# Copying the last depthwise unit of a chunk in two halves, and letting the first scores wait for the first half alone

## The chip, the cores and the metric

The kernel runs on one core of one Trainium2 chip. The metric is device time in microseconds (us) of that core; lower is better. All arithmetic is float32. Five queues of instructions run side by side and meet at semaphores: PE (TensorE, matmuls; PEld in the views is its weight load), ACT (ScalarE), DVE (VectorE), POOL (GpSimd, which only clears one small tile here) and SP (SyncE, which issues the transfers). Each executes its own instructions in the order written.

## The reference, cut to what matters

The input is x of (4, 64, 128, 128). It is group-normalised (32 groups of 2 channels), goes through a windowed channel attention, and is added back:

```python
x + attention(_gn(x))
qkv = einsum('bchw,oc->bohw', x, w_qkv) + b_qkv           # 64 -> 192 channels
qkv = depthwise_3x3(qkv, w_dw) + b_dw                     # padded by 1
# windows of 8x8 pixels, 4 heads of 16 channels, pixels flattened to 64
attn = softmax(einsum('nhcx,nhdx->nhcd', q, k) * temperature)
out  = einsum('nhcd,nhdx->nhcx', attn, v)
gate = gelu(einsum('nhcx,yx->nhcy', v, w_mlp) + b_mlp)
out  = einsum('bchw,oc->bohw', unwindow(out * gate), w_proj) + b_proj
```

## The kernel before, in words

Two images at a time fill the 128 partitions, so there are two pairs of images, each cut into 8 bands of 16 rows: 16 chunks. A chunk has 16 columns of windows, and one window column stands for 4 "patches" of the tile `qkv` (2 rows of windows by 2 images), 64 patches in all. A chunk is worked off in four steps of 4 window columns (16 patches) each; the step has number i, the chunk is i // 4, and a = i % 4 is the place in the chunk. There are 64 steps.

The work on a chunk has two layers, and the kernel does both at once.

**The lower layer makes q, k and v of the next chunk.** It is cut into 22 units. Sixteen `mix` units (8 in step a=0, 8 in step a=1; `mix_channels`, matmuls of L672) multiply the normalised patches by the 64 to 192 channel weights. Six `dw` units (three in step a=2, three in step a=3; `depthwise`, matmuls of L707) apply the 3x3 filter as a 64-column matmul per channel, 32 matmuls to a unit. A unit writes one of two PSUM buffers of two banks each (`work`; units take them in turn), raises `full` of the buffer, is copied to SBUF, and the copy raises `free`. The copies are `evacuate_mix` (to `z`) and `evacuate_dw` (to `qkv`), on ACT except for one unit per chunk. Units 0 and 1 of `dw` hold v, 2 and 3 hold q, 4 and 5 hold k: unit 5 brings 16 of the channels of k for all 64 patches, and is the last of the chunk. It is in the second buffer, which the unit after the next one, mix 1 of the following chunk, takes again.

**The upper layer is the attention of the current chunk**, one step at a time: `score` (L744, 64x64 products of q and k), on DVE the mask, the maximum and its subtraction (L511, L516, L518), on ACT the exponential (`exponent`, L341), on DVE sum, reciprocal, product and transpose (L532 to L543); `turn_v` (L777, a transpose of v) with its copy on ACT (`v_up`, L347); `gates` (L765) for two steps at a time with `gate_up` on DVE (L525) and `gelu` on ACT (L351); `apply_probs` (L793), `mix` on DVE (L503), `project` (L804) and `residual` (L552).

The order of each engine is written out by hand. At a chunk's start PE does this: `depthwise` of units 4 and 5 of the coming chunk, `apply_probs` of the last step, `qkv_of` (two waits: units 4 and 5 are copied), `score` of step a=0, mix 0 and mix 1, `project` of the step before, `turn_v`, mix 2 to mix 5, `gates`, `apply_probs`, mix 6 and 7. In the very first step, mix 0, mix 1 and the gates stand between `qkv_of` and `score`.

ACT does in step a=3: the exponential, the copy of unit 3, `v_up`, the table of Gelu, the Gelu of one step, the copy of unit 4, the Gelu of a second step, the copy of unit 5, and the table of the exponential (`exp_table`, L356: the load and a one-element activation). Then in step a=0: the copies of mix 0 and mix 1, the exponential, `v_up`, and the copies of mix 2 to 5. A Gelu and an exponential need different tables, so each change costs an ACT_TABLE_LOAD.

For the first chunk (n = 0) units 0, 2 and 4 are copied by ACT and 1, 3 and 5 by DVE (L417 is its copy helper, L326 that of ACT). The semaphores that the change touches are `free[1]`, raised by the copy of unit 5, and a new one.

Of the kernel before, what the change touches and what calls it, by code (L numbers as in the profile page):

```python
# [26 lines left out]
NW = 4 * COLS  # L27
BATCH = 4
BATCHES = COLS // BATCH
# [12 lines left out]
SPLIT = 16  # L42
# [44 lines left out]
def gates_in(i):  # L87

    return (i + 2, i + 3) if i % 2 == 0 and i + 2 < STEPS else ()


def gelus_in(i):

    a = i % BATCHES
    return (0, 1) if i == 0 else (i, i + 1) if a == 2 else gates_in(i - 1) if a == 3 else ()
# [7 lines left out]
def build(nc, x, taps, hot, edges, weights, out):  # L103
    with ExitStack() as ctx:
        def sb(name, shape, dt=F32):
            return ctx.enter_context(nc.sbuf_tensor(name, shape, dt))
# [4 lines left out]
        def sem(name):  # L111
            return ctx.enter_context(nc.semaphore(name))

        z = sb("z", [P, QKV, NW])
        dw = sb("dw", [P, QKV, HW])
        qkv = sb("qkv", [P, 2, 3, NW, HALF])
# [19 lines left out]
        at = [sum(sizes[:n]) for n in range(len(sizes) + 1)]  # L136
# [11 lines left out]
        work = [unit_ps[:, 0:2], unit_ps[:, 2:4]]  # L148
# [19 lines left out]
        free = [sem("free0"), sem("free1")]  # L168
# [9 lines left out]
        deviated = sem("deviated")  # L178
        seen_done = sem("seen_done")
        patches_ready = sem("patches_ready")  # L180
        gate_done = sem("gate_done")
        scores_done = sem("scores_done")
        v_t_done = sem("v_t_done")
# [21 lines left out]
        def wait_full(engine, unit):  # L205
            engine.wait_ge(full[number[unit] % 2], number[unit] // 2 + 1)

        def wait_free(engine, unit):
            engine.wait_ge(free[number[unit] % 2], number[unit] // 2 + 1)

        def buffer(unit):
            return number[unit] % 2
# [5 lines left out]
        def evacuate_first(engine, copy, g):  # L218

            engine.wait_ge(first_full[g % 4], g // 4 + 1)  # L220
            copy(z[0:NPATCH, :, 4 * g:4 * g + 4].rearrange("p c (b t) -> p c b t", t=2),
                 quarter[g % 4][0:NPATCH, :, 0:2 * QKV].rearrange("p t (b c) -> p c b t", b=2)
                 ).then_inc(first_free[g % 4], 1)

        def evacuate_mix(engine, copy, n, g):

            unit = ("mix", n, g)
            wait_full(engine, unit)
            copy(z[0:NPATCH, :, 4 * g:4 * g + 4].rearrange("p c (b t) -> p c b t", t=2),
                 work[buffer(unit)][0:NPATCH, :, 0:2 * QKV].rearrange("p t (b c) -> p c b t", b=2)  # L230
                 ).then_inc(free[buffer(unit)], 1)

        def evacuate_dw(engine, copy, n, v):

            unit = ("dw", n, v)
            if n > 1:
                engine.wait_ge(v_t_done, (n - 1) * BATCHES)
            wait_full(engine, unit)
            kind, at = kind_of(v)
            copy(qkv[:, n % 2, kind, :, at:at + SPLIT],  # L240
                 work[buffer(unit)][:].rearrange("p a (c w) -> p w (a c)", w=NW)
                 ).then_inc(free[buffer(unit)], 1)

        def kind_of(v):
            return (2, 0, 1)[v // (HALF // SPLIT)], v % (HALF // SPLIT) * SPLIT
# [73 lines left out]
        @block.scalar  # L319
        def _(act):  # L320
            act.dma_start(tap_w[:], taps).then_inc(taps_in, 16)
            act.dma_start(hot_b, hot).then_inc(hot_in, 16)
            act.dma_start(consts[:], weights).then_inc(consts_in, 16)

            def copy(to, of):
                return nc.scalar.activation(to, of, ACT.Copy)  # L326

            def evacuate_build(m):

                act.wait_ge(built, m + 1)  # L330
                px = PX * TILES
                copy(dw[0:K, :, m * px:(m + 1) * px].rearrange("p c (r x) -> p c r x", x=PX),
                     banks[m % 2][0:K, :, 0:PX * QKV].rearrange("p r (x c) -> p c r x", x=PX)).then_inc(dw_ready, 1)

            def deviation(pair):
                wait_free(act, ("var", pair))
                nc.scalar.activation(small[:, 3:4], small[:, 2:3], ACT.Sqrt).then_inc(deviated, 1)

            def exponent(i):
                act.wait_ge(shifted, i + 1)  # L340
                nc.scalar.activation(scores[:], scores[:], ACT.Exp).then_inc(exp_ready, 1)  # L341

            def v_up(i):
                act.wait_ge(v_t_done, i + 1)
                if i:
                    act.wait_ge(mix_done, i)
                nc.scalar.activation(v_t[:], turn_ps, ACT.Copy).then_inc(v_t_ready, 1)  # L347

            def gelu(j):
                act.wait_ge(gate_biased, j + 1)  # L350
                nc.scalar.activation(gate[:, j % GATES], gate[:, j % GATES], ACT.Gelu).then_inc(gate_ready, 1)  # L351

            def exp_table(k):
                if k:
                    act.wait_ge(table_loaded, k)
                nc.scalar.activation(small[:, 7:8], zeros[:, 0:1], ACT.Exp).then_inc(table_loaded, 1)  # L356

            for m in range(BUILDS):
                evacuate_build(m)
            act.wait_ge(zeroed, 1)  # L360
            nc.scalar.activation(small[:, 6:7], zeros[:, 0:1], ACT.Sqrt)
            act.wait_ge(x_in[0], 16)
            act.wait_ge(x_in[1], 16)
            copy(T[:, 1:, 1:1 + W], loaded[:, 0:BAND + 1]).then_inc(first_copied, 1)
            deviation(0)
            exp_table(0)
            for g in range(0, COLS, 2):
                evacuate_first(act, copy, g)
            for v in range(0, 6, 2):
                evacuate_dw(act, copy, 0, v)  # L370
            tables = 1
            for i in range(STEPS):
                n, a = i // BATCHES + 1, i % BATCHES
                more = n < CHUNKS
                if a < 2:
                    if more:
                        evacuate_mix(act, copy, n, 8 * a)
                        evacuate_mix(act, copy, n, 8 * a + 1)
                    exponent(i)
                    v_up(i)  # L380
                    if more:
                        for g in range(8 * a + 2, 8 * a + 6):
                            evacuate_mix(act, copy, n, g)
                if a == 2:
                    v_up(i)
                    exponent(i)
                    if more:
                        evacuate_dw(act, copy, n, 0)
                if a == 3:
                    exponent(i)  # L390
                    if more:
                        evacuate_dw(act, copy, n, 3)
                    v_up(i)
                if (n, a) == (BANDS - 1, 2):
                    deviation(1)
                now = gelus_in(i)
                for j in now:
                    gelu(j)
                    if more and a == 3 and j == now[0]:
                        evacuate_dw(act, copy, n, 4)  # L400
                if more and a == 3:
                    evacuate_dw(act, copy, n, 5)
                if now:
                    exp_table(tables)
                    tables += 1
                if more and a == 2:
                    evacuate_dw(act, copy, n, 2)
                if more and a < 2:
                    evacuate_mix(act, copy, n, 8 * a + 6)
                    evacuate_mix(act, copy, n, 8 * a + 7)  # L410
# [209 lines left out]
        def _(pe):  # L620
# [101 lines left out]
            def qkv_of(n):  # L722

                wait_free(pe, ("dw", n, 4))
                wait_free(pe, ("dw", n, 5))

            def windows(i, g):
                at = 4 * (i % BATCHES * BATCH + g)
# [94 lines left out]
            for i in range(STEPS):  # L823
                units_now = fillers(i)
                cut = (2, 6) if i % BATCHES < 2 else (i % BATCHES - 2, 3)
                if i % BATCHES == 0:
                    qkv_of(i // BATCHES)
                if i == 0:
                    fill(units_now[:cut[0]])
                    gates(0, 0)  # L830
                    gates(1, 0)
                score(i)
                if i:
                    fill(units_now[:cut[0]])
                    project(i - 1)
                turn_v(i)
                fill(units_now[cut[0]:cut[1]])
                for j in gates_in(i):
                    gates(j, i)
                apply_probs(i)  # L840
                fill(units_now[cut[1]:])
# [85 lines left out]
```

## Time and profile before

| | |
|---|---|
| median of 3 runs | 691.59 us (689.6, 691.59, 695.38) |
| the profiled execution: time | 692.99 us |
| the profiled execution: span | 690.9 us, mean granted TensorE clock 0.981 |
| PE busy | 617.4 us, 89% |
| DVE busy | 509.6 us, 74% |
| ACT busy | 479.8 us, 69% |
| ACT copies of `mix` units (L326) | 244 of 809 ns |
| ACT copies of `dw` units (L326) | 78 of 1014 ns |

The span is from the first to the last instruction; the time adds what lies around it (2.1 us here). PE is the engine with the largest share. The busy shares are averages over 16 chunks, so they don't tell which engine sets the time at a given place; the chain of waits and the timelines at a chunk's start do.

### The profile page before, as it was taken

How to read it: one execution, taken by the hardware profiler on the slowest of the kernel's cores; microseconds unless marked ns; L12 is line 12 of the kernel's file. 1: busy time of each engine (PE TensorE's matmuls, PEld its weight loads, DVE VectorE, ACT ScalarE, POOL GpSimd, SP SyncE). 2: the span in 40 equal slices, each digit the busy share in tenths (PEclk: the TensorE clock that was granted, in tenths of full speed). 3: DMA queues.
4: the chain of work that ended last, by engine and by line, in shares of the span. 5: the costliest groups of instructions: out<-in, count | busy, mean ns of one | idle time of the engine just before them, and what ended most of it. 6: DMA issues, size and time to landing. Idle time of an engine off the chain costs nothing.

```text
span 690.9 us, 32466 instructions
## 1 busy us (share of the span) xinstructions
PE 617.4 (89%) x15044; PEld 541.4 (78%) x15044; DVE 509.6 (74%) x790; ACT 479.8 (69%) x631; POOL 0.3 (0%) x5
## 2 busy tenths in 40 slices
PE   3787899999999999999999999989899999999854
PEld 2686688888878788878878797878879788878743
DVE  4874678888878888777868776777768667777674
ACT  3642868777867768776867768776777768776722
POOL 0000000000000000000000000000000000000000
PEclk9999999999999999999999999999999999999985
DMA  9872116243350714141230505041140504111032
GB/s 363 254 217 67 32 50 218 70 153 121 95 194 19 239 50 149 61 135 57 58 138 4 193 4 195 3 131 66 47 151 5 194 4 150 42 64 64 4 90 34
DMA packets 29240, 72.28 MB, mean 105 GB/s; under 512 B 9801, under 2 KB 16329, under 8 KB 24233
## 3 DMA queue, kind: packets, MB, share of 16 engines
q1 hardware_dynamic: 28674, 68.57, 30.6%
q8 instruction: 118, 1.93, 1.2%
q10 hardware_dynamic: 432, 1.65, 0.6%
q14 instruction: 16, 0.13, 0.1%
HBM read 53.44 MB, written 16.78 MB: 102 GB/s over the span
## 4 chain that ended last, share of the span: by engine, by line
PE 84%; ACT 6%; issue 5%; DVE 3%; DMA 1%; ACTq 0%; DVEq 0%
PE unit_ps L707 27%; PE unit_ps L672 24%; PE rest_ps L804 10%; PE rest_ps L744 6%; PE rest_ps L793 6%; PE rest_ps L765 5%; ACT z L326 4%; PE rest_ps L777 4%; DMA patches<-in_hot 1%; ACT dw L326 1%; PE rest_ps L641 1%; PE rest_ps L672 1%; PE unit_ps L634 0%; DVE neg_max L516 0%; DVE scores L511 0%
## 5 line engine op out<-in xcount | busy, mean ns | idle before, releaser
L326 ACT ACTIVATE z<-unit_ps 100x768 f32<-100x768 f32 x244 | 184.9, 809 | 68.6 <-PE unit_ps L672 68.4
L672 PE MATMUL unit_ps<-consts,patches 64*100 64x192 f32 x1984 | 194.3, 335 | 13.1 <-ACT z L326 11.0
L707 PE MATMUL unit_ps<-z,dw 103*64 103x64 f32 (+2 forms) x6144 | 190.8, 223 | 7.8 <-issue 6.6
L707 PEld LDWEIGHTS unit_ps<-z,dw 103*64 103x64 f32 (+2 forms) x6144 | 183.7, 138 | 15.0 <-issue 14.0
L672 PEld LDWEIGHTS unit_ps<-consts,patches 64*100 64x100 f32 x1984 | 151.2, 163 | 35.9 <-ACT z L326 20.7
L326 ACT ACTIVATE qkv<-unit_ps 128x1024 f32<-128x1024 f32 x78 | 79.1, 1014 | 21.9 <-PE unit_ps L707 21.9
L503 DVE TENSOR_TENSOR gate<-rest_ps,gate 128x512 f32<-128x512 f32 x64 | 44.1, 689 | 61.1 <-PE rest_ps L793 57.9
L341 ACT ACTIVATE scores<-scores 128x512 f32<-128x512 f32 x64 | 40.5, 632 | 58.1 <-DVE scores L518 56.5
L511 DVE TENSOR_TENSOR scores<-rest_ps,consts 128x512 f32<-128x512 f32 x64 | 44.2, 690 | 45.1 <-PE rest_ps L744 44.8
L804 PE MATMUL rest_ps<-gate,consts 128*128 128x256 f32 x256 | 75.2, 417 | 1.4 <-DVE gate L503 0.8
L552 DVE SCALAR_TENSOR_TENSOR staged<-rest_ps,consts,staged 128x512 f32<-128x512 f32 x64 | 48.0, 750 | 26.6 <-PE rest_ps L804 26.6
L744 PE MATMUL rest_ps<-qkv 64*64 64x64 f32 x2048 | 47.1, 227 | 17.7 <-issue 17.7
L744 PEld LDWEIGHTS rest_ps<-qkv 64*64 64x64 f32 x2048 | 38.9, 138 | 27.1 <-issue 27.1
L347 ACT ACTIVATE v_t<-rest_ps 128x512 f32<-128x512 f32 x64 | 38.1, 596 | 30.4 <-PE rest_ps L777 27.4
L804 PEld LDWEIGHTS rest_ps<-gate,consts 128*128 128x128 f32 x256 | 44.8, 195 | 15.1 <-issue 7.2
L793 PE MATMUL rest_ps<-v_t,probs_t 64*64 64x64 f32 x2048 | 46.0, 227 | 10.8 <-DVE probs_t L543 10.2
L793 PEld LDWEIGHTS rest_ps<-v_t,probs_t 64*64 64x64 f32 x2048 | 38.8, 138 | 17.6 <-issue 16.3
L543 DVE STREAM_TRANSPOSE probs_t<-scores 128x512 f32<-128x512 f32 x64 | 45.5, 711 | 2.2
L518 DVE TENSOR_TENSOR scores<-scores,neg_max 128x512 f32<-128x512 f32 x64 | 44.3, 692 | 2.2
L536 DVE TENSOR_TENSOR scores<-scores,inv_total 128x512 f32<-128x512 f32 x64 | 44.3, 692 | 2.2
L516 DVE TENSOR_REDUCE neg_max<-scores 128x8 f32<-128x512 f32 x64 | 43.9, 686 | 2.2
L525 DVE TENSOR_TENSOR gate<-rest_ps,consts 128x512 f32<-128x512 f32 x64 | 43.6, 682 | 2.3 <-PE rest_ps L765 2.3
(55 smaller groups left out, 513.8 us busy)
## 6 DMA issues: line engine op xcount, KB each, us to landing
staged<-in_x SPq DMA_DIRECT2D x17, 1024.0 KB, 5.0
out_y<-staged SPq DMA_DIRECT2D x15, 1024.0 KB, 5.4
T<-in_x SPq DMA_DIRECT2D x12, 1152.0 KB, 6.7
seen<-in_x SPq DMA_DIRECT2D x32, 256.0 KB, 3.4
qkv<-in_x SPq DMA_DIRECT2D x6, 1024.0 KB, 13.9
T<-in_x SPq DMA_DIRECT2D x3, 1088.0 KB, 6.1
staged<-in_x SPq DMA_DIRECT2D x2, 512.0 KB, 23.2
out_y<-staged SPq DMA_DIRECT2D x4, 256.0 KB, 3.0
```

The costliest lines, as they stand in the source:

```text
L326: return nc.scalar.activation(to, of, ACT.Copy)
L503: nc.vector.tensor_tensor(held, pair_ps[:, :, 0:BATCH * HW], held, ALU.mult).then_inc(mixed_ready, 1)
L511: nc.vector.tensor_tensor(scores[:].rearrange("p (h g) d -> p h g d", h=2), score_ps[:, :, 0:BATCH * C].rearrange("p h (g d) -> p h g d", ...
L518: nc.vector.tensor_tensor(scores[:], scores[:], neg_max[:].unsqueeze(2).to_broadcast([P, WIDE, C]), ALU.add).then_inc(shifted, 1)
L536: nc.vector.tensor_tensor(scores[:], scores[:], inv_total[:].unsqueeze(2).to_broadcast([P, WIDE, C]), ALU.mult).then_inc(probs_ready, 1)
L543: nc.vector.transpose(probs_t[:].rearrange("p w d -> p (w d)"), scores[:].rearrange("p w d -> p (w d)")).then_inc(probs_t_ready, 1)
L552: nc.vector.scalar_tensor_tensor(to, proj_ps.rearrange("p (r c) -> p r c", r=BAND), b_proj, to, op0=ALU.add, op1=ALU.add).then_inc(out_rea ...
L672: last = nc.tensor.matmul(to[0:NPATCH, t, b * QKV:(b + 1) * QKV], patches[image, b, g], w1[image], start=True, stop=True)
L707: last = nc.tensor.matmul(to[h * HW:(h + 1) * HW, m // 8, m % 8 * NW:(m % 8 + 1) * NW], dw[0:used, c, :], z[0:used, c, :], start=True, sto ...
L744: last = nc.tensor.matmul(score_ps[pair, h ^ b, g * C:(g + 1) * C], q[rows, pair], k[rows, pair], start=True, stop=True)
L793: last = nc.tensor.matmul(pair_ps[side(b, h), b, g * HW:(g + 1) * HW], probs_t[rows, (h ^ b) * BATCH + g, :], v_t[rows, at], start=True, s ...
L804: last = nc.tensor.matmul(proj_ps[:, b * 4 * HW:(b + 1) * 4 * HW], proj[:, b * P:(b + 1) * P], gate[:, i % GATES, b].rearrange("p g (r c) ...
```

## The change

The copy of unit 5 becomes two copies. The first takes patches 0 to 31 of the 64 (the patches of steps a=0 and a=1), the second patches 32 to 63 (steps a=2 and a=3). Each half is 128 partitions by 512 elements instead of 1024. The first half raises a new semaphore, `first_columns`; the second raises `free` of the buffer, as the whole copy did. On ACT the first half is put ahead of the second Gelu of step a=3, with the wait for unit 5, and the second half stands where the whole copy stood. For chunk 0, DVE does the two halves one behind the other. On PE, `qkv_of` waits for `first_columns` in place of `free`, and step a=2 of each chunk gets a wait for the whole unit.

```diff
@@ in the semaphores
+        first_columns = sem("first_columns")
@@ evacuate_dw
             wait_full(engine, unit)
+            for part in (0, 1) if v == 5 else (None,):
+                dw_part(copy, n, v, part)
+
+        def dw_part(copy, n, v, part):
+
+            unit = ("dw", n, v)
             kind, at = kind_of(v)
-            copy(qkv[:, n % 2, kind, :, at:at + SPLIT],
-                 work[buffer(unit)][:].rearrange("p a (c w) -> p w (a c)", w=NW)
-                 ).then_inc(free[buffer(unit)], 1)
+            which = slice(0, NW) if part is None else slice(part * NW // 2, (part + 1) * NW // 2)
+            done = first_columns if part == 0 else free[buffer(unit)]
+            copy(qkv[:, n % 2, kind, which, at:at + SPLIT],
+                 work[buffer(unit)][:].rearrange("p a (c w) -> p w (a c)", w=NW)[:, which]).then_inc(done, 1)
@@ ACT, step a=3
                     gelu(j)
                     if more and a == 3 and j == now[0]:
                         evacuate_dw(act, copy, n, 4)
+                        wait_full(act, ("dw", n, 5))
+                        dw_part(copy, n, 5, 0)
                 if more and a == 3:
-                    evacuate_dw(act, copy, n, 5)
+                    dw_part(copy, n, 5, 1)
@@ PE, qkv_of
                 wait_free(pe, ("dw", n, 4))
-                wait_free(pe, ("dw", n, 5))
+                pe.wait_ge(first_columns, n + 1)
@@ PE, the loop over steps
                 if i % BATCHES == 0:
                     qkv_of(i // BATCHES)
+                if i % BATCHES == 2:
+                    wait_free(pe, ("dw", i // BATCHES, 5))
```

## Rows read from the trace of the kernel before

**Rows 1.** The page: busy time and share of PE, and the chain by engine.
```profile
PE 617.4 (89%) x15044; PEld 541.4 (78%) x15044; DVE 509.6 (74%) x790; ACT 479.8 (69%) x631; POOL 0.3 (0%) x5
PE 84%; ACT 6%; issue 5%; DVE 3%; DMA 1%; ACTq 0%; DVEq 0%
```

**Rows 2.** The view of waits: total us, times, longest us.
```profile
PE rest_ps L744 <- issue: 17.7, 21, 1.4
```

**Rows 3.** Timeline of PE, one chunk's start: start, us, operation, [idle before].
```profile
218.95 3.95 PE L707 MATMUL unit_ps<-z,dw 103*64 103x64 f32 x128
222.83 0.69 PE L793 MATMUL rest_ps<-v_t,probs_t 64*64 64x64 f32 x32
224.13 0.69 PE L744 MATMUL rest_ps<-qkv 64*64 64x64 f32 x32 [0.61 <-issue]
224.76 1.55 PE L672 MATMUL unit_ps<-consts,patches 64*100 64x192 f32 x16
...
227.20 0.60 PE L777 MATMUL rest_ps<-consts,qkv 128*128 128x128 f32 x4
227.73 1.55 PE L672 MATMUL unit_ps<-consts,patches 64*100 64x192 f32 x16
229.54 1.60 PE L672 MATMUL unit_ps<-consts,patches 64*100 64x192 f32 x16 [0.26 <-ACT z L326]
```

**Rows 4.** Timeline of ACT, the same chunk's start.
```profile
221.50 1.01 ACT L326 ACTIVATE qkv<-unit_ps 128x1024 f32<-128x1024 f32 x1
222.41 0.62 ACT L351 ACTIVATE gate<-gate 128x512 f32<-128x512 f32 x1
223.01 1.03 ACT L326 ACTIVATE qkv<-unit_ps 128x1024 f32<-128x1024 f32 x1
224.05 1.28 ACT L356 ACT_TABLE_LOAD   x1
225.35 0.20 ACT L356 ACTIVATE small<-zeros 128x1 f32<-128x1 f32 x1
225.70 1.51 ACT L326 ACTIVATE z<-unit_ps 100x768 f32<-100x768 f32 x2 [0.15 <-PE unit_ps L672]
227.10 0.63 ACT L341 ACTIVATE scores<-scores 128x512 f32<-128x512 f32 x1
227.84 0.60 ACT L347 ACTIVATE v_t<-rest_ps 128x512 f32<-128x512 f32 x1
228.68 1.51 ACT L326 ACTIVATE z<-unit_ps 100x768 f32<-100x768 f32 x2 [0.24 <-PE unit_ps L672]
```

**Rows 5.** Timeline of DVE, the same chunk's start.
```profile
224.89 0.69 DVE L511 TENSOR_TENSOR scores<-rest_ps,consts 128x512 f32<-128x512 f32 x1 [0.42 <-PE rest_ps L744]
...
226.33 0.69 DVE L518 TENSOR_TENSOR scores<-scores,neg_max 128x512 f32<-128x512 f32 x1
```

**Rows 6.** Timeline of PE and ACT at the start of the chunk before.
```profile
178.31 3.95 PE L707 MATMUL unit_ps<-z,dw 103*64 103x64 f32 x128
...
182.60 0.62 ACT L351 ACTIVATE gate<-gate 128x512 f32<-128x512 f32 x1
...
184.23 0.69 PE L744 MATMUL rest_ps<-qkv 64*64 64x64 f32 x32 [1.35 <-issue]
```

**Rows 7.** Timeline of DVE and PE at the first step of all.
```profile
61.72 1.22 DVE L417 COPY qkv<-unit_ps 128x1024 f32<-128x1024 f32 x1 [4.66 <-PE unit_ps L707]
63.04 1.55 PE L672 MATMUL unit_ps<-consts,patches 64*100 64x192 f32 x16 [1.37 <-issue]
```

**Rows 8.** Groups by line and shape: count, busy us, mean ns, idle before.
```profile
L326 ACT ACTIVATE qkv<-unit_ps 128x1024 f32<-128x1024 f32 x78 | 79.1, 1014 | 21.9 <-PE unit_ps L707 21.9
L347 ACT ACTIVATE v_t<-rest_ps 128x512 f32<-128x512 f32 x64 | 38.1, 596 | 30.4 <-PE rest_ps L777 27.4
```

**Rows 9.** Timeline of PE: the shortest and longest idle inside a score.
```profile
136.46 0.44 PE L744 MATMUL rest_ps<-qkv 64*64 64x64 f32 x10 [0.37 <-issue]
...
488.65 0.38 PE L744 MATMUL rest_ps<-qkv 64*64 64x64 f32 x9 [1.41 <-issue]
```

## The prediction, made before the changed kernel was run

> **What bounds the kernel now.** I began with the page. PE is busy 89% of the span and makes 84% of the chain that ended last; ACT has 6% of that chain and plain "issue" 5% [rows 1]. So time is won where PE stands still, and nearly nowhere else. The view of waits gives PE's idle time ahead of the score matmuls: 17.7 us in 21 places, longest 1.4 [rows 2]. The timeline shows what these are. Fifteen are chunk starts, the wait of `qkv_of` for the copy of unit 5: ten of 0.55 to 0.71 us (I call them **short**) and five of 1.34 or 1.35 us (**long**); the others lie inside a score and no copy ends them [rows 9]. A sixteenth start, that of the first chunk, shows as 1.37 us ahead of mix 0 [rows 7]. The releaser is printed as "issue", so I matched it by time: ACT's copy of unit 5 runs 223.01 to 224.04, and the score begins 0.09 us behind it, at 224.13 [rows 3, 4].
>
> Then I followed the short start further, since a wait that goes is worth only what the next one leaves. PE has 0.26 us of idle time ahead of mix 4, at 229.54, for ACT's copy of mix 2 [rows 3]. ACT copied that at 228.68, having waited 0.24 us for PE [rows 4]. The two engines are nearly tied there: PE's gain must also be had on ACT.
>
> **The long starts** differ on PE's side alone. Unit 5 is finished at 178.31 + 3.95 = 182.26, 0.34 us before ACT begins its second Gelu at 182.60 [rows 6]. In the short start it is finished at 218.95 + 3.95 = 222.90, while that Gelu (222.41 to 223.03) is running [rows 3, 4].
>
> **The change, part by part.**
>
> *Price of a half.* No row shows a half of this copy. The nearest is ACT's PSUM copy of the same shape, 128x512, at 0.60 us; the whole is 1.01 us [rows 8]. The bounds are 0.51 us (half of the whole) and 1.01 us (no cheaper than the whole). I take 0.60. ACT's successive activations overlap by 0.10 us: the copy at 221.50 lasts 1.01, but the Gelu behind it starts at 222.41 [rows 4]. So two halves occupy ACT for 0.50 + 0.60 = 1.10 against 1.01, 0.09 more.
>
> The Trainium skill speaks against such a split: "Advanced Engine Details and Errata", section "The Read-Write Bubble", says that the memory latency stands as a bubble between instructions of ScalarE and advises tiles of 512 or 1024 elements, so the half is still of a size that it allows. The trace disagrees for these sizes: activations overlap instead [rows 4]. By the page's rule the 0.10 of overlap would go at each of the two new joints, which is the rival of the joints below.
>
> *Short start, PE.* The first half waits for unit 5 (222.90), begins 0.03 later at 222.93 and ends 223.53; with the same 0.09, the score begins at 223.62 instead of 224.13: 0.51 earlier. `apply_probs` ends at 222.83 + 0.69 = 223.52, so no more was there to have.
>
> *Short start, ACT.* This is the cost. ACT now stands idle from 222.51 to 222.93, where it had a Gelu to do; what is queued behind the wait is that Gelu, the second half, the table load and the whole of step a=0. The Gelu starts at 223.43, the second half 0.52 later at 223.95, ending 224.55; the table load starts 0.51 us later than the 224.05 of before. Its 1.28 and the small activation end at 226.06; mix 0's copy, overlapped by 0.10, starts at 225.96 (before 225.70), the exponential 1.40 later at 227.36, `v_up` 0.53 later at 227.89, and mix 2's copy 0.50 later at 228.39. Before it was 228.68, because it stood waiting for PE three times: 0.15 and 0.24 in the rows, and the 0.11 between the exponential's end (227.73) and `v_up`, which began behind `turn_v` (227.20 + 0.60) [rows 3, 4]. PE is ready with mix 2 about 0.51 earlier than 228.68, at 228.17, and so does not bind. Mix 4 starts 0.29 us earlier: of PE's 0.51, ACT lets 0.29 through.
>
> *What else might bind there.* Mix 1 takes unit 5's buffer: it needs the second half (224.55) and begins at about 224.76 - 0.51 + 0.78 = 225.03, so no wait. DVE idled 0.42 ahead of the mask, so this can move up by 0.42; the subtraction then ends at 226.33 + 0.69 - 0.42 = 226.60, well before 227.36 [rows 5]. The delayed Gelu belongs to the step after next.
>
> *Long start.* The first half takes the Gelu's place at 182.60, ends 183.20, and the score starts at 183.29 instead of 184.23: 0.94 earlier. The Gelu starts at 183.10, the second half ends at 184.23, and the table load is only 0.1 us late (0.09, the price of the split). Along the same chain as above, ACT's slack of about 0.80 (0.25 + 0.21 + 0.34, the three waits with their overlaps) less this 0.09 leaves mix 4 earlier by 0.71. The last chunk start is a long one with no mix units behind it; the mask follows the score directly, and I count the full 0.94.
>
> *First start.* DVE's copy takes 1.22 us [rows 7]; scaled as ACT's (0.596/1.014) a half is 0.72, so mix 0, on the chain, starts 0.50 earlier. Bounds: 0.61 and nothing.
>
> *The other edits.* The additional wait of step a=2 is for a copy that ended some 20 us before; PE's queue of matmuls covers it, and uncovered it would cost at most the 0.09 seen above, 1.4 us over 16 chunks. No transfer is issued or moved. SP waits for unit 5 to be full, which nothing touches.
>
> **The sum.** 10 x 0.29 + 4 x 0.71 + 0.94 + 0.50 = 7.2 us. Against the profiled execution's own 692.99 that gives 685.8. That execution was 1.4 us above the median of 691.59; the median becomes **684.4 us**.
>
> **The rivals.**
>
> *Slower: ACT pays for the split.* A strided half copy could cost more than 0.60. Each x us more per half delays the table load by 2x, and with it mix 2's copy. A short start turns into a loss at x = 0.15. With the small differences at the ends left out, the sum is 7.2 - 30x, so the kernel is slower from x = 0.24 (a half of 0.84). At the bound of 1.01, 10 x (-0.53) + 4 x (-0.11) + 0.53 + 0 = -5.2: 696.8 us. Against it: the group of 128x512 [rows 8]. For it: that copy reads PSUM in order, and this one in strides. Chance 0.08, of which half with something besides that takes it past 1%.
>
> *The joints.* The two new joints (first half to Gelu, Gelu to second half) don't overlap by the 0.10 of the old ones: 0.2 us later per start, 15 x 0.2 = 3.0 off the sum, 4.2 left, 687.4 us. Every pair of activations in [rows 4] that doesn't wait speaks against it; only the untried shape speaks for it. Chance 0.08. (The Trainium skill's section on the bubble, above, would have it so.)
>
> *The stalls take it back.* PE stands still in 11 other places with no releaser, 0.37 to 1.41 us each; the two ends of those inside scores are in [rows 9]. If the instruction supply lies behind them and catches up during the idle time I remove, they grow. At worst by all that is saved, no change, 691.6; I put this case at half of it, 688. For it: the stalls come at like places of the program. Against: their lengths follow no pattern of the waits before them. Chance 0.18.
>
> The Trainium skill, "Runtime: NRT & Kernel Launch", section "Instruction fetch mechanics", says that fetching runs ahead in blocks and is mostly hidden. By that the stalls aren't fetching, and the sum stands at 7.2; the rows show idle time that I can't name, so I keep the case.
>
> *Nothing arrives.* The half doesn't release the score, or a tie I haven't seen ahead of the next chunk (DVE in step a=3) holds the old pace: 691. Chance 0.06.
>
> *ACT lets it all through.* If ACT's chain has more overlap than I counted, the short starts give 0.51 and the long 0.94: 10 x 0.51 + 5 x 0.94 + 0.50 = 10.3, 681.3 us. Chance 0.10.
>
> **How the numbers follow.** My forecast has 0.50. A measurement of this kernel can tell about 1%, 6.9 us, from no change; 7.2 is barely beyond, so I split the forecast's chance, 0.29 beyond and 0.21 within. Faster by over 1%: 0.29 + 0.10 = 0.39. Slower by over 1%: 0.04. I raise this to 0.06 for what I don't see, out of the middle, which keeps 0.55. The range takes in the forecast, the full gain, the joints, the stalls and most of no change: 681 to 691.5. Outside are the slower case and the tails.
>
> **What would show it.** In the changed trace: L326 with shape 128x512 at about 600 ns, 30 of them (15 starts, two each); idle ahead of the score below 0.15 us in short starts and about 0.4 in long ones; the table load at a short start some 0.95 us behind the start of the score, where it now starts 0.08 before it; idle of PE ahead of mix 4 up from 0.26 to about 0.5, put down to ACT's copy of `z`; the waits of ACT at mix 0 and mix 2 gone. Halves of 0.8 us would prove me wrong on the price; starts as foreseen with a chunk as long as before, on the clipping downstream.

## The result and the profile after

The changed kernel takes **684.14 us** (median of 4 runs, 683.18 to 685.65) against 690.9 us for the kernel before beside it (median of 4, 689.6 to 695.38): a ratio of 0.9893, 95% interval [0.9844, 0.9942]. A second series gave 684.55 against 692.26, 0.9888 [0.9859, 0.9917]. So the gain is 1.1%, small, but both intervals exclude no change. The forecast was 684.4. The profiled execution took 683.18 us, with a span of 681.4 against 690.9.

The page of the changed kernel, parts 1 and 4 (line numbers have moved by 8 to 10: ACT's copy helper is L334, the score L754, the unit 5 matmuls L717, mix L682, the exponential's table L364):

```profile
PE 616.7 (91%) x15044; PEld 540.8 (79%) x15044; DVE 510.3 (75%) x791; ACT 476.3 (70%) x646; POOL 0.3 (0%) x5
...
PE 67%; ACT 21%; DVE 6%; issue 4%; DMA 1%; ACTq 0%; DVEq 0%
```

PE's work is nearly the same (617.4 and 616.7 us busy); it stands idle 9 us less. ACT's share of the chain went from 6% to 21%: the chain now runs through ACT at each chunk start [rows 1].

The view of waits. First the row of the kernel before for PE's wait ahead of mix units (for ACT's copy to `z`), then the changed kernel's row for it and the one that answers to [rows 2]:

```profile
PE unit_ps L672 <- ACT z L326: 11.0, 31, 2.1
```

```profile
PE unit_ps L682 <- ACT z L334: 13.9, 31, 2.0
...
PE rest_ps L754 <- issue: 6.1, 10, 1.9
```

The idle time ahead of scores fell from 17.7 us in 21 places to 6.1 in 10. The one ahead of mix units rose from 11.0 us in 31 places to 13.9 in 31: 2.9 us came back as a wait for ACT, 0.17 at each of the fourteen starts with mix units behind them and 0.5 in the second step of all.

Timelines of PE and of ACT at the start that answers to [rows 3] and [rows 4], a short one:

```profile
217.97 3.95 PE L717 MATMUL unit_ps<-z,dw 103*64 103x64 f32 x128
...
222.66 0.69 PE L754 MATMUL rest_ps<-qkv 64*64 64x64 f32 x32
...
228.24 1.60 PE L682 MATMUL unit_ps<-consts,patches 64*100 64x192 f32 x16 [0.43 <-ACT z L334]
```

```profile
220.52 1.01 ACT L334 ACTIVATE qkv<-unit_ps 128x1024 f32<-128x1024 f32 x1
221.97 0.60 ACT L334 ACTIVATE qkv<-unit_ps 128x512 f32<-128x512 f32 x1 [0.44 <-PE unit_ps L717]
222.46 0.62 ACT L359 ACTIVATE gate<-gate 128x512 f32<-128x512 f32 x1
222.98 0.59 ACT L334 ACTIVATE qkv<-unit_ps 128x512 f32<-128x512 f32 x1
223.59 1.28 ACT L364 ACT_TABLE_LOAD   x1
...
224.99 1.50 ACT L334 ACTIVATE z<-unit_ps 100x768 f32<-100x768 f32 x2
226.37 0.63 ACT L349 ACTIVATE scores<-scores 128x512 f32<-128x512 f32 x1
226.89 0.60 ACT L355 ACTIVATE v_t<-rest_ps 128x512 f32<-128x512 f32 x1
227.37 1.52 ACT L334 ACTIVATE z<-unit_ps 100x768 f32<-100x768 f32 x2
```

Unit 5 is finished at 217.97 + 3.95 = 221.92. I measure from there: the score begins 0.74 us later (before: 1.23) and mix 4 6.32 later (before: 6.64). The idle time ahead of the score is gone, all of ACT's waits between the second half and mix 2's copy are gone, and PE waits 0.43 us ahead of mix 4 instead of 0.26. The chain of waits says the same; over this stretch it is ACT alone:

```profile
221.97 0.60 ACT qkv L334
222.56 0.52 ACT gate L359
223.08 0.49 ACT qkv L334
...
223.59 1.28 ACT L364
...
226.48 0.52 ACT scores L349
227.00 0.49 ACT v_t L355
227.49 0.71 ACT z L334
```

A long start, PE, to be held against [rows 6] (unit 5 was finished at 180.96):

```profile
181.98 0.69 PE L754 MATMUL rest_ps<-qkv 64*64 64x64 f32 x32 [0.40 <-issue]
...
187.56 0.73 PE L682 MATMUL unit_ps<-consts,patches 64*100 64x192 f32 x6 [0.43 <-ACT z L334]
```

Score and mix 4 come 1.02 and 6.60 us behind the unit's end; before it was 1.97 and 7.38. The first start, PE, to be held against [rows 7]:

```profile
62.36 1.55 PE L682 MATMUL unit_ps<-consts,patches 64*100 64x192 f32 x16 [0.84 <-issue]
```

The groups of unit 5's halves, on ACT and on DVE (rows 8 have the 128x1024 at 1014 ns):

```profile
L334 ACT ACTIVATE qkv<-unit_ps 128x512 f32<-128x512 f32 x30 | 17.8, 593 | 2.8 <-PE unit_ps L717 2.7
L427 DVE COPY qkv<-unit_ps 128x512 f32<-128x512 f32 x2 | 1.3, 685 | 4.4 <-PE unit_ps L717 4.4
```

**The account.** Ten short starts at 0.34 (mean over them), four long ones at 0.78, the last one 0.92 at the score, the first one 0.53: 3.4 + 3.1 + 0.9 + 0.5 = 7.9 us. The two spans differ by 9.5. The stalls that no copy ends sum to 9.6 us in the first profile of before and 8.3 here, 1.3 less; whether the change has a part in that is taken up below. Against this, the 0.53 of the first start was taken back right behind it. PE, before, then changed, from the first step to the mix unit in the second step ahead of which PE stands 0.26 us:

```profile
70.26 2.62 PE L672 MATMUL unit_ps<-consts,patches 64*100 64x192 f32 x16 [2.05 <-ACT z L326]
...
83.30 1.60 PE L672 MATMUL unit_ps<-consts,patches 64*100 64x192 f32 x16 [0.26 <-ACT z L326]
```

```profile
78.54 2.07 PE L814 MATMUL rest_ps<-gate,consts 128*128 128x256 f32 x4
...
83.21 1.60 PE L682 MATMUL unit_ps<-consts,patches 64*100 64x192 f32 x16 [0.26 <-ACT z L334]
```

From mix 0 to that unit it is 83.30 - 63.04 = 20.26 us before and 83.21 - 62.36 = 20.85 here: 0.6 lost. Both kernels have a spell at the lower clock there, which stretches the group at 70.26 from 1.60 to 2.62 and the one at 78.54 from 1.13 to 2.07, but it falls in different places (view by stretches, before, then changed; the granted clock is the third number from the end):

```profile
72.00:74.00 2.00, 2.00 (x50) 1.50 (x51) 0.62 (x2) 1.51 (x3) 0.00 (x0) 0.50 0.48 113
```

```profile
78.00:80.00 2.00, 2.00 (x10) 1.25 (x7) 0.00 (x0) 1.84 (x3) 0.00 (x0) 0.50 0.00 0
```

In the kernel before PE's groups are longer by 1.5 us in the spell, but PE stands ahead of its next wait for ACT, which shrinks by 0.5 (1.41 us ahead of the mix unit at 78.46; 1.92 in the changed kernel, at 76.76). In the changed kernel they are longer by 1.7 us, behind that wait, and nothing covers it. What places the spell stays open: the split in place, below, has the same instructions in these two steps and took 19.37. So: 7.9 at the starts, 1.3 in the stalls, 0.15 ahead of the first start, less 0.6, make 8.8 of the 9.5; the rest is in pieces too small to place.

### The profile page after: what moved, and what is told of

Read it like the earlier page. It is cut to its first block, busy times and chain, and to the rows that moved or that the text cites. A ratio compares the mean times of both kernels' runs of the same rounds, so it can differ in the third digit from the quotient of the medians.

```text
span 681.4 us, 32484 instructions
## 1 busy us (share of the span) xinstructions
PE 616.7 (91%) x15044; PEld 540.8 (79%) x15044; DVE 510.3 (75%) x791; ACT 476.3 (70%) x646; POOL 0.3 (0%) x5
## 4 chain that ended last, share of the span: by engine, by line
PE 67%; ACT 21%; DVE 6%; issue 4%; DMA 1%; ACTq 0%; DVEq 0%
PE unit_ps L717 22%; PE unit_ps L682 19%; PE rest_ps L814 7%; ACT z L334 7%; PE rest_ps L775 5%; PE rest_ps L803 4%; PE rest_ps L754 4%; ACT qkv L334 4%; ACT L364 3%; PE rest_ps L787 3%; ACT gate L359 2%; ACT v_t L355 2%; DMA patches<-in_hot 1%; ACT dw L334 1%; ACT scores L349 1%
## 5 line engine op out<-in xcount | busy, mean ns | idle before, releaser
L334 ACT ACTIVATE z<-unit_ps 100x768 f32<-100x768 f32 x244 | 184.7, 809 | 62.7 <-PE unit_ps L682 62.5
L682 PE MATMUL unit_ps<-consts,patches 64*100 64x192 f32 x1984 | 193.5, 334 | 15.4 <-ACT z L334 13.9
L717 PE MATMUL unit_ps<-z,dw 103*64 103x64 f32 (+2 forms) x6144 | 190.6, 223 | 6.9 <-issue 5.6
L717 PEld LDWEIGHTS unit_ps<-z,dw 103*64 103x64 f32 (+2 forms) x6144 | 183.5, 138 | 14.0 <-issue 13.0
L682 PEld LDWEIGHTS unit_ps<-consts,patches 64*100 64x100 f32 x1984 | 150.5, 162 | 38.4 <-ACT z L334 23.6
L334 ACT ACTIVATE qkv<-unit_ps 128x1024 f32<-128x1024 f32 (+1 forms) x93 | 81.0, 877 | 24.5 <-PE unit_ps L717 24.4
L754 PE MATMUL rest_ps<-qkv 64*64 64x64 f32 x2048 | 47.1, 227 | 7.4 <-issue 6.1
L754 PEld LDWEIGHTS rest_ps<-qkv 64*64 64x64 f32 x2048 | 39.0, 138 | 16.8 <-issue 14.2
L542 DVE TENSOR_REDUCE total<-scores 128x8 f32<-128x512 f32 x64 | 43.6, 681 | 6.5 <-ACT scores L349 5.8
```

The costliest lines, as they stand in the source:

```text
L682: last = nc.tensor.matmul(to[0:NPATCH, t, b * QKV:(b + 1) * QKV], patches[image, b, g], w1[image], start=True, stop=True)
L717: last = nc.tensor.matmul(to[h * HW:(h + 1) * HW, m // 8, m % 8 * NW:(m % 8 + 1) * NW], dw[0:used, c, :], z[0:used, c, :], start=True, sto ...
L754: last = nc.tensor.matmul(score_ps[pair, h ^ b, g * C:(g + 1) * C], q[rows, pair], k[rows, pair], start=True, stop=True)
```

## The experiments

All ratios are to the kernel before, run on the same chip in the same series. There are three series, with medians of the kernel before of 690.9 us (the changed kernel's row), 691.62 (order alone to v_t later) and 692.26 (the rows with "again" and the quarter). In the table "score" and "mix 4" are the times from the end of unit 5 to each, in the profile, for a short and a long start.

| kernel | median, us | ratio, 95% | short: score, mix 4 | long: score, mix 4 |
|---|---|---|---|---|
| before | 690.9 | 1 | 1.23, 6.64 | 1.97, 7.38 |
| changed | 684.14 | 0.9893 [0.9844, 0.9942] | 0.74, 6.32 | 1.02, 6.60 |
| order alone | 689.06 | 0.9952 [0.9926, 0.9978] | 1.23, 6.64 | 1.45, 6.85 |
| split in place | 684.79 | 0.9901 [0.9868, 0.9934] | 0.81, 6.22 | 1.54, 6.94 |
| cost alone | 696.56 | 1.0075 [1.005, 1.01] | 1.75, 7.16 | 2.03, 7.44 |
| v_t later | 680.67 | 0.9857 [0.9818, 0.9896] | 0.74, 6.15 | 1.02, 6.42 |
| v_t later, again | 681.31 | 0.9842 [0.9815, 0.987] | 0.74, 6.15 | 1.01, 6.42 |
| quarter first | 679.6 | 0.9816 [0.9789, 0.9843] | 0.53, 5.94 | 0.81, 6.21 |
| changed, again | 684.55 | 0.9888 [0.9859, 0.9917] | 0.75, 6.32 | 1.02, 6.60 |
| before, again | 691.6 | 1.0006 [0.9978, 1.0034] | 1.23, 6.64 | 1.97, 7.38 |

### The order alone

This edit and the next two are to the changed kernel; "..." stands for lines left out. Here unit 5 is copied whole, ahead of the second Gelu.

```diff
-            for part in (0, 1) if v == 5 else (None,):
+            for part in (None,):
...
                         evacuate_dw(act, copy, n, 4)
-                        wait_full(act, ("dw", n, 5))
-                        dw_part(copy, n, 5, 0)
-                if more and a == 3:
-                    dw_part(copy, n, 5, 1)
+                        evacuate_dw(act, copy, n, 5)
...
-                pe.wait_ge(first_columns, n + 1)
+                wait_free(pe, ("dw", n, 5))
...
-                if i % BATCHES == 2:
-                    wait_free(pe, ("dw", i // BATCHES, 5))
```

> Unit 5 is copied whole, ahead of the second Gelu; the scores wait for the whole copy. This tells the move ahead of the Gelu from the split. My theory (PE gains what the score's release comes earlier, capped by ACT's slack of some 0.80 us up to mix 2's copy): in a short start the copy can begin only at the end of unit 5, score 0.10 earlier, mix 4 0.10 earlier; in a long start the copy takes the Gelu's place, score and mix 4 0.5 earlier. First start unchanged. Sum 10 x 0.10 + 5 x 0.53 = 3.7 us faster than the kernel before, about 687. Rival (the split is what pays, the order does nothing): 691. Rival (the order is all of it): 683 to 684.

Measured: 0.9952, that is 3.3 us faster (1.5 to 5.1) for 3.7 expected. Long starts gained 0.52 at the score and 0.53 at mix 4, as expected. Short starts gained 0.02 in the mean over the ten, nothing at the one shown, where I had 0.10. ACT and PE at a short start:

```profile
222.96 1.02 ACT L334 ACTIVATE qkv<-unit_ps 128x1024 f32<-128x1024 f32 x1 [0.50 <-PE unit_ps L714]
```

```profile
224.08 0.69 PE L751 MATMUL rest_ps<-qkv 64*64 64x64 f32 x32 [0.60 <-issue]
```

The unit was finished at 219.82 + 3.03 = 222.85 and the copy began 0.11 behind it, which is where the copy of the kernel before stood as well (223.01 for 222.90): there it waited for the unit and not for the Gelu. The order pays only where the unit is finished early; it isn't all of the gain, so that rival falls.

The 0.11 itself is worth a look. At the first of the ten short starts (unit finished at 105.49) the copy begins 0.05 behind the unit and the score comes 1.17 behind it, not 1.23. `evacuate_dw` has one wait there; for every later chunk it has a second one, for `v_t_done`, ahead of the wait for the unit. The changed kernel's first half has the wait for the unit by itself, and begins 0.05 behind the unit in every short start. So of its 0.49 at the score, 1.03 - 0.60 = 0.43 is the shorter copy and 0.06 the earlier beginning. No run takes the second wait alone out; that the 0.06 is its price is inferred.

### The split in place

Both halves are copied behind the second Gelu, one behind the other.

```diff
                         evacuate_dw(act, copy, n, 4)
-                        wait_full(act, ("dw", n, 5))
-                        dw_part(copy, n, 5, 0)
                 if more and a == 3:
-                    dw_part(copy, n, 5, 1)
+                    evacuate_dw(act, copy, n, 5)
```

> Two halves, both behind the second Gelu, where the whole copy stood; the scores wait for the first half. This tells the split from the move. My theory: the score comes 0.42 earlier in short and in long starts alike, and ACT is only 0.09 late, so all 0.42 reach mix 4 (the idle time ahead of the score is then 0.2 in short and 0.9 in long starts). Sum 15 x 0.42 + 0.5 for the first start = 6.8 us, about 684. Rival (ACT's chain to mix 2's copy takes its toll whatever the order, 0.2 us per start): 4 us, 687. Rival (the move is what pays): 690.

Measured: 0.9901, 6.8 us faster, as expected. Short starts gained 0.42 at the score and at mix 4, long ones 0.43 and 0.44. Everything reached mix 4, since ACT has no new wait and keeps its slack. ACT and PE:

```profile
222.96 1.08 ACT L334 ACTIVATE qkv<-unit_ps 128x512 f32<-128x512 f32 x2
...
228.19 1.51 ACT L334 ACTIVATE z<-unit_ps 100x768 f32<-100x768 f32 x2 [0.24 <-PE unit_ps L680]
```

```profile
223.65 0.69 PE L752 MATMUL rest_ps<-qkv 64*64 64x64 f32 x32 [0.18 <-issue]
...
229.06 1.11 PE L680 MATMUL unit_ps<-consts,patches 64*100 64x192 f32 x10 [0.26 <-ACT z L334]
```

ACT's waits of 0.24 ahead of mix 2's copy and PE's of 0.26 ahead of mix 4 are those of the kernel before [rows 3, 4]. This kernel and the changed one can't be told apart in time (0.9901 and 0.9893, intervals overlapping), and the starts say why: against the split in place, the move ahead of the Gelu loses 0.10 in each of ten short starts and wins 0.34 in each of four long ones and 0.51 at the last, some 0.9 us in all. The split makes the gain; the move adds little to it, and less than these runs can show.

### The cost alone

```diff
-                pe.wait_ge(first_columns, n + 1)
+                wait_free(pe, ("dw", n, 5))
...
-                if i % BATCHES == 2:
-                    wait_free(pe, ("dw", i // BATCHES, 5))
```

> Copies as in the changed kernel (first half ahead of the second Gelu), but PE waits for the second half, as before the change for the whole. This shows the cost of the change on ACT without its gain. My theory: in a short start the second half ends 0.5 us later than the whole copy did, and the score with it; in a long start 0.1 later. Score and table load are then again together, so nothing is hidden: 10 x 0.5 + 5 x 0.1 + 0.2 = 5.7 us slower than the kernel before, 696 to 697. Rival (ACT has slack ahead of the score as well): 691.

Measured: 1.0075, 5.2 us slower (3.5 to 6.9) for 5.7 expected, with the score 0.52 later in short starts and 0.06 in long ones. PE at a short start:

```profile
223.09 0.69 PE L754 MATMUL rest_ps<-qkv 64*64 64x64 f32 x32 [1.12 <-issue]
```

So the price that I put on ACT's chain is real and is paid in the changed kernel too. There it falls into ACT's slack, because PE no longer waits for the second half.

### v_t behind mix 2 and mix 3

This is the changed kernel with one more edit on ACT.

```diff
                     exponent(i)
-                    v_up(i)
+                    if a or not more:
+                        v_up(i)
                     if more:
                         for g in range(8 * a + 2, 8 * a + 6):
                             evacuate_mix(act, copy, n, g)
+                            if a == 0 and g == 3:
+                                v_up(i)
```

> The changed kernel, and in step a=0 ACT copies mix 2 and mix 3 ahead of v_t instead of behind it. In the changed kernel PE stands 0.43 us ahead of mix 4 for ACT's copy of mix 2. My theory (ACT's order up to that copy clips the gain): the copy comes up to 0.24 us earlier, when PE has mix 2 ready; PE's idle time ahead of mix 4 falls to the 0.26 of the kernel before; 15 x 0.17 = 2.5 us faster than the changed kernel, about 681.5. Rival (the 0.43 is made of PE's own products, as the 0.26 of step a=1): no change, 684. Rival on the other side: v_t is late for the gates of step a=0, PE waits there: 684 to 687.

> The changed kernel with v_t copied behind mix 2 and mix 3 in step a=0, once more, beside the changed kernel on the same chip. Expected again 2 to 4 us faster than the changed kernel: 2.5 us by the idle time ahead of mix 4 (15 x 0.17). If the 680.7 of its first run was a lucky one, it comes out within 1 us of the changed kernel.

Measured: 0.9857 and 0.9842, against 0.9893 and 0.9888 for the changed kernel; beside the latter on one chip 681.31 against 684.55, 3.2 us faster for 2.5 expected. ACT and PE at a short start:

```profile
227.30 1.51 ACT L334 ACTIVATE z<-unit_ps 100x768 f32<-100x768 f32 x2 [0.21 <-PE unit_ps L685]
228.70 0.60 ACT L355 ACTIVATE v_t<-rest_ps 128x512 f32<-128x512 f32 x1
```

```profile
228.16 1.60 PE L685 MATMUL unit_ps<-consts,patches 64*100 64x192 f32 x16 [0.26 <-ACT z L334]
229.69 1.16 PE L778 MATMUL rest_ps<-consts,qkv 64*64 64x64 f32 x64
```

The copy of mix 2 waits for PE again, PE's idle time is back at 0.26, and mix 4 comes 0.17 earlier in short starts and 0.18 in long ones. The gates (L778) begin without idle time, so v_t isn't late. In the first step of all, too, PE's wait ahead of mix 4 fell, from 2.05 us to 1.56. Over all starts that makes 14 x 0.17 + 0.5 = 2.9 us. This shows that ACT's order was what clipped the gain: score to mix 4 is 5.40 us here and in the kernel before, and 5.58 in the changed one.

### A quarter first

This is the kernel of the last section with a smaller first part.

```diff
-            which = ... slice(part * NW // 2, (part + 1) * NW // 2)
+            which = ... slice(0, NW // 4) if part == 0 else slice(NW // 4, NW)
...
-                if i % BATCHES == 2:
+                if i % BATCHES == 1:
                     wait_free(pe, ("dw", i // BATCHES, 5))
```

> As e5, but the first part is the 16 patches of step a=0 alone (128x256), the second the other 48 (128x768), and PE waits for the whole unit in step a=1. My theory: the first part takes about 0.40 us instead of 0.60; in a short start the score then comes only 0.1 earlier, since apply_probs ends there, in a long start 0.2 earlier; ACT's sum is unchanged. 10 x 0.1 + 5 x 0.2 + 0.3 for the first start = 2.3 us faster than e5, some 678.5. Rival (what is left is ACT's chain, which a smaller first part doesn't shorten): same as e5. Rival on the other side: the longer second part keeps the second Gelu and the table load no later, but a part of 256 costs nearly as much as one of 512: no gain, up to 1 us slower.

Measured: 679.6 us, 0.9816 [0.9789, 0.9843]. The interval lies below that of the changed kernel (0.9888 [0.9859, 0.9917], same series), so this beats both kernels. Its interval overlaps that of the kernel with halves and v_t later ([0.9815, 0.987]), but both carry the spread of the kernel before. The two set side by side, in the same series, are 678.64 to 680.44 us in 5 runs and 680.32 to 682.85 in 6: the means differ by 1.7 us (0.7 to 2.8), for 2.3 expected. ACT and PE at a short start:

```profile
221.52 0.38 ACT L334 ACTIVATE qkv<-unit_ps 128x256 f32<-128x256 f32 x1 [0.37 <-PE unit_ps L720]
221.80 0.62 ACT L359 ACTIVATE gate<-gate 128x512 f32<-128x512 f32 x1
222.32 0.80 ACT L334 ACTIVATE qkv<-unit_ps 128x768 f32<-128x768 f32 x1
```

```profile
221.41 0.69 PE L806 MATMUL rest_ps<-v_t,probs_t 64*64 64x64 f32 x32
222.00 0.69 PE L757 MATMUL rest_ps<-qkv 64*64 64x64 f32 x32
```

The score came 0.21 earlier in both kinds of start, where I had expected 0.1 in the short ones. I had taken the printed end of `apply_probs` as a floor (here 221.41 + 0.69 = 222.10), but PE's groups are printed overlapped by some 0.1, and the score begins at 222.00.

### Both kernels once more

> The kernel before once more, for a second profile. PE's idle time with no releaser in 11 places away from the chunk starts differed between the profiles so far. If it belongs to the execution and not to the kernel, the places are the same as in the first profile (same count of matmuls behind them) and the lengths are others, by some tenths each and by 1 to 2 us in the sum. If it belongs to the kernel, lengths and sum repeat to a tenth. Time 690 to 692 either way.

> The changed kernel once more, for a second profile and a closer ratio. The chunk starts give 8.0 us between the two first profiles; the other 1.5 us of the 9.5 between those spans I put down to the unnamed stalls. If that is right, short and long starts repeat to 0.05 us, the stalls don't, and the ratio comes out at 0.988 to 0.990 (8.0 of 691 is 1.16%). If the stalls really shrank with the change, their sum is again 1.5 us below that of the kernel before and the ratio is near 0.986.

The starts of the changed kernel repeat to 0.02 us, but for one mix 4 at 6.37 instead of 6.32. Those of the kernel before repeat less well: seven of its fifteen scores moved by 0.04 to 0.67 us, as I read it because a stall earlier in the chunk shifts PE against ACT; one long start of 1.97 became 1.30 where a stall of 0.40 fell into units 4 and 5. So the starts of this second pair sum to 7.6 us; the spans, 688.5 and 681.1, differ by 7.4. The stretch behind the first start took 19.24 and 20.84 us, 1.6 lost this time.

The stalls. The first row of [rows 9], 0.37 us, has its like in the second profile of before; then the two rows of the changed kernel's profiles at a stall in unit 3 of a later chunk (a matmul of the program is two records in the traces, so the 32 of a unit are 64):

```profile
135.86 0.44 PE L744 MATMUL rest_ps<-qkv 64*64 64x64 f32 x10 [1.40 <-issue]
```

```profile
331.31 1.27 PE L717 MATMUL unit_ps<-z,dw 109*64 109x64 f32 x37 [0.47 <-issue]
```

```profile
330.60 1.27 PE L717 MATMUL unit_ps<-z,dw 109*64 109x64 f32 x37 [1.23 <-issue]
```

The place is the same (10 records of the score left, 37 up to the unit's end), the length isn't: 0.37 and 1.40, 0.47 and 1.23. Most places repeat so, and two of before's second profile have no like in its first.

The places go with the program: 15 records are left at the stall at 368.22 of the changed kernel and at its like in all kernels with the additional wait of step a=2, 11 in those without. And they lie on a grid: counted in records, the stalls of before stand 888, 894, 1397, 511 and 894 apart, which is 7, 7, 11, 4 and 7 times about 127, and so on to the end. The first of these is one that neither the prediction nor the sums below count: 1.92 us at 58.53, in the middle of a unit of the first chunk (1.59 in the second profile, 1.62 in both of the changed kernel).

Summed over rows of more than 0.15 us, the stalls are 9.6 and 9.0 us in the kernel before and 8.3 and 8.3 in the changed one; in the other kernels, in the order of the table, 7.3 (order alone), 8.3, 9.4, 9.0, 9.1 and 8.6. The two sums of before differ by 0.6, less than the 1 to 2 that I expected. The kernel with hardly any gain at the short starts has the lowest sum, the quickest one in the starts, the quarter, has 8.6. So they don't take the saved time back. Whether the change makes them 0.9 us shorter can't be said from two profiles each; the ratio of the second series (0.9888, 7.7 us, interval 5.7 to 9.8) has room for the starts with it and without.

## Why the prediction was right

**The price of a half** was 0.593 us on ACT (forecast 0.60) and 0.685 on DVE (forecast 0.72). Activations overlapped at the new joints: 221.97 to 222.46 and 222.46 to 222.98 in the changed trace, for activations of 0.60 and 0.62. The rival of the joints and the slower rival fall with that; the cost alone measured 0.52 per short start, for which the forecast had 0.51.

**Short starts**: 0.49 at the score (forecast 0.51) and 0.32 at mix 4 (0.29); the mean of ten is 0.34. **Long starts**: 0.95 and 0.78 (0.94 and 0.71). From the first half to mix 2's copy ACT took 5.40 us where 5.46 was worked out; half of that is the exponential and v_t's copy, which occupy it 0.52 and 0.48 us rather than 0.53 and 0.50. The table load came 0.93 us behind the start of the score (forecast 0.95). **The last start** gave 0.92 (0.94) and **the first** 0.53 (0.50). The sum of the starts is 7.9 us for a forecast 7.2, in the second pair of profiles 7.6. That the median, 684.14, lies 0.3 us from the forecast is in part luck: the runs of one kernel lie 2 to 6 us apart, and the starts gave more than forecast while the stretch behind the first one took 0.6 to 1.6 back.

**The clipping** was the step that made the number: without it the forecast would have been 10.3 us. It was shown twice, by the idle time ahead of mix 4 (0.43, forecast about 0.5) and by the kernel that takes v_t out of the way and gets 0.17 per start back.

**What was off.** "No more was there to have" at the short starts was wrong: the quarter had 0.21 more, and its score begins 0.1 ahead of the printed end of `apply_probs`. The 0.10 expected of the order alone at short starts didn't come. That a spell at the lower clock falls differently in the first two steps, and takes back as much as the first start gives, has no term in the sum. And I charged the move ahead of the Gelu with its costs without asking what the split would give if left in place: the answer, 0.9901, is the same within the measurement, and 0.9 us less by the starts.

**The stalls**, given a chance of 0.18, neither took anything back nor added anything that could be shown. What they are stays open. **The clock** is the same in the mean (0.981 in both profiles), but not in place: its spell in the first two steps is what moved the 0.6 us, and 1.6 in the second pair.

The Trainium skill's page "Advanced Engine Details and Errata" ("The Read-Write Bubble") would have had a bubble at each joint; at 512 elements none showed. Its page "Runtime: NRT & Kernel Launch" ("Instruction fetch mechanics") says that instructions are fetched in blocks of 256 and that this is mostly hidden. The grid of the stalls fits such blocks: 127 matmul records with their weight loads (PE and PEld both count x15044) are 254 instructions, and the waits add a few. So the prediction took too much from the page when it read "mostly hidden" as "the stalls aren't fetching"; that they are is a likely reading, and no run shows it.

## What to carry to other kernels

When a consumer needs only part of what a long copy brings, let it wait for that part; the price is the fixed part of one more instruction, here 0.1 us of ACT for 0.4 to 0.5 us of PE at the score. Then follow the engine that copies up to its next meeting with the consumer: its slack there (here 0.80 us) caps the gain, and work that nobody waits for yet (here v_t) should stand behind that meeting. Before moving an instruction ahead of another, look at whether its input is there: where it wasn't, the move cost 0.1 us, where it was, it brought 0.34.

## What the runs showed of the hardware

An ACT copy out of PSUM took 0.380, 0.593, 0.805 and 1.012 us for 256, 512, 768 and 1024 elements per partition: 0.82 us per 1000 elements and 0.17 fixed, of which 0.10 is hidden behind the activation before. DVE's took 0.425, 0.685, 0.948 and 1.225.

In the profile of the quarter, one stall of 2.08 us ahead of a matmul at 192.82 was followed by a spell at the lower clock. The view by stretches (busy time of PE, PEld, DVE, ACT, POOL, then the granted clock, the DMA share and GB/s):

```profile
192.00:194.00 2.00, 1.18 (x17) 1.07 (x18) 0.69 (x1) 0.00 (x0) 0.00 (x0) 0.83 0.88 260
194.00:196.00 2.00, 2.00 (x15) 1.44 (x11) 1.38 (x2) 0.81 (x1) 0.00 (x0) 0.50 0.69 287
196.00:198.00 2.00, 2.00 (x11) 1.62 (x12) 0.52 (x1) 1.42 (x3) 0.00 (x0) 0.82 0.02 4
```

0.50 is the lower level, 1.2 GHz. From the end of that stall to the mix unit of the same step ahead of which PE stands 0.26 us, PE took 199.61 - 192.82 = 6.79 us; in the second profile of v_t later the same stretch took 5.16, behind a stall of 1.48. That is 1.6 us against the 3.2 that the quarter's fifteen starts gained (0.21 each), and part of why its span (677.5) was only 0.9 us below that one's (678.4). The like stall was followed by such a spell in the split in place (1.63 us) and by none in the changed kernel (1.91 us; clock 1.00 all along), so the length of the stall doesn't decide it by itself.
